# New instruction order and PSUM placement in the attention pass of a macaron layer (slot-routed FFN, delta-rule attention, FFN again)

## Chip, cores and metric

One core of a Trainium2 chip. The metric is the device time of the whole program in microseconds (us).

## What is computed

`x` is (2, 4096, 512), all float32. Three stages, of which the kernel makes three passes:

```python
x = x + 0.5 * ffn(layernorm(x))     # FFN: 64 slots, top-8 routing, a GRU step on the slots
x = x + attention(layernorm(x))       # 16 heads of 32; below x is the normed tile
x = x + 0.5 * ffn(layernorm(x))
# attention, 16 heads of 32, for every position t:
q, k = l2norm(x @ Wq), l2norm(x @ Wk);  v = x @ Wv
alpha, beta = sigmoid(x @ Wa + ba), sigmoid(x @ Wb + bb)
state = alpha * state + outer(k, beta * (v - k @ state));  y = q @ state
y = rmsnorm(y, g_norm) * silu(x @ Wg);  return y @ Wo
```

The kernel does the attention in chunks of 32 positions (the four chunks of a 128-row tile side by side on the partitions), with a 32x32 unit-triangular matrix per head and chunk that is inverted on VectorE, and one 32x32 state product per head from chunk to chunk. Note: the pass also adds the first FFN's output to x before attention, and does the routing of the second FFN (its layer norm, logits, top 8, slot sums) behind it.

## The kernel before

Rows are taken in 32 tiles of 128 positions for each of the 2 batches; a function's arguments are (tile n, batch b, part). There are four stretches: routing of the first FFN (to about 309.7 us), the attention pass (309.7 to about 2880 us), a short GRU stage (`mid`), and the last sum with the output.

The attention pass is software-pipelined over tiles and its order is written out by hand, one list for each engine: a fill (`first_pe`, `first_act`, `first_pool`, `first_dve`, `first_sp`), a steady step called once per tile, and a drain (`last_...`). Engines meet only through semaphores, and each runs its own list strictly in order. A step works on tile p (adding the FFN, transposing, projecting), on q = p - 1 (32x32 products and inversion), on r = q - 1 (state chain, output product, second routing) and on s = r - 1 (slot sums). What matters for the steps below:

- TensorE, 128-wide products: `proj_k`, `proj_q` (4 parts each per batch, one 128x512 product a part, L899 through `project`), `proj_va` (keys of 128x288), `proj_vb`, `proj_g` (L954), `out_proj` (L1101), `hidden`, `ffn` (L886), `slots`, `qe_T`, transposes.
- TensorE, 32x32 products, always 16 of them to a piece and 4 of them side by side in the array: `gram` (L994), `apply_uw` (L1018), `apply_gy` (eight pieces for each batch; a half with 8 products on L1060, which waits for `gq_turn`, and a half with 8 products on L1069, which waits for `y1_turn`), `chain` (L1082, four links for each batch). In the trace each float32 product stands as two matmul records, so a half of an `apply_gy` piece is x16.
- ScalarE copies results out of PSUM: `move_uw` (L2166) after `apply_uw`, `move_gq` (L2172) after the fourth and the eighth piece of `apply_gy`, `move_va`, squares, `gate_of`.
- VectorE: `chunk_kept` (L3280) after `move_gq`; `state` (L3286), the transpose between two chain links; `query_scale` (L3225), `reading` (L3254), `invert` (L3267 and L3269, 30 rounds in ten calls), `first_sum` (L3168), `second_sum` (L3297, reads the output product), `last_top` and `last_weights` (routing).
- GpSimd: masks, decays, norms' powers, `slot_add` (L2718).
- The sync engine's queue (SP): the matrix to be inverted goes out to DRAM and comes back in another layout (`coupling_out`, `coupling_in`), the inverse likewise (`inverse_out` L531, `inverse_in` L537, from which `apply_uw` reads); `load_alpha` (L494) brings the routing weights for `ffn`.

PSUM has 8 banks of 128x512; each result has a bank (the lists `..._at`), and `free(...)` in front of a product waits until the last reader of that bank's previous content is done. Thus `proj_va(n, 0)` writes bank 3, which `out_proj(n-2, 1)` had, and waits for `x2`, the signal of `second_sum(n-2, 1)`:

```python
if part == 0:
    pe.wait_ge(S["xnT"], both(n, b))
    if b == 0:
        free((n - 2, (S["x2"], both(n - 2, 1))), (n - 1, (T["pt"][1], nth(n - 1, 1))))
```

In the steady list before, the pieces of `apply_gy` of batch 0 stand as six at the end of a step and two at the start of the next, with nothing between them.

Of the kernel before, what the change touches and what calls it, by code (L numbers as in the profile page):

```python
# [3876 lines left out]
```

How the kernel before makes its waits and increments, by code:

```python
            def __call__(self, ins):  # L238
                ins.then_inc(self.sem, 1)
                self.n += 1
                self.e.wait_ge(self.sem, self.base + self.n)
# [99 lines left out]
        def mid(e, m):  # L341
# [10 lines left out]
                def gate_product(dst, j, c, n):  # L352
                    for k in range(KC):
                        if j == 0 and k % 2 == 0:
                            e.wait_ge(mid_act, o_act + 1 + k // 2)
                        last = mm(dst, giT[:, k * P:(k + 1) * P], wihT_at(k, j)[:, c:c + n], start=(k == 0), stop=(k == KC - 1))
                    last.then_inc(mid_pe, 1)
                def value(k):
                    return mm(Bk[1][:, :], hTT[:, k * P:(k + 1) * P], voT_at(k), start=(k == 0), stop=(k == KC - 1))
                e.wait_ge(mid_dve, o_dve + 1)
                turn(0)
                e.wait_ge(mid_dve, o_dve + 2)
                turn(1)
                if m == 1:
                    e.wait_ge(wih_in, RELOAD)
                gate_product(A[0][:, :], 0, 0, D)
                e.wait_ge(aT, NT * (m + 1))
                gate_product(C[0][:, :], 2, 0, D)
                gate_product(z_at[0], 1, 0, HC)
                gate_product(z_at[1], 1, HC, HC)
                e.wait_ge(mid_dve, o_dve + 7)
                turn(0)
                e.wait_ge(mid_act, o_act + 7)
                value(0)
                e.wait_ge(mid_dve, o_dve + 8)
                turn(1)
                value(1)
                e.wait_ge(mid_act, o_act + 8)
```

## Time and profile before

| | |
|---|---|
| median of 3 runs | 2947.53 us (2940.21 to 2959.49) |
| span of the profiled execution | 2958.8 us |
| slowest of the 3 runs | 2959.49 us |
| TensorE matmul busy | 2700.6 us (91%) |
| VectorE, ScalarE, GpSimd busy | 1882.3, 1059.9, 1328.6 us |
| attention pass, first to last `ffn` product | 309.7 to 2706.5 us |

The span runs from the first to the last instruction of one execution; 2959.49 us is the run that stands nearest to it, 0.7 us above, and the profile does not name a time of its own beside the span. A row of a group of instructions gives line, engine, operation, output and inputs, shape and count, then busy time, mean length of one (ns), and the engine's idle time just before them with what ended it; "issue" is idle time for which the profile shows no cause.

### The profile page before, as it was taken

What the parts mean: (1) busy time and instruction counts of PE and PEld (TensorE: products, weight loads), DVE (VectorE), ACT (ScalarE), POOL (GpSimd) and SP (SyncE); (2) the same over time, 40 slices, a digit from 0 to 9 for tenths busy, and PEclk for the clock granted to TensorE, in tenths of its full rate; (3) what the DMA queues carried; (4) which work ended last, traced back from release to release, by engine and by line L of the source; (5) the groups of instructions that cost most, each with busy time, mean ns of one, the idle gap of its engine ahead of it and who ended that gap; (6) DMA issues with size and microseconds to landing.
All of it is one profiled execution on the core that took longest, in us unless ns stands there. A gap on an engine that the chain in (4) does not pass through costs nothing. (4 is left out here: it accounts for less than half of the span.)

```text
span 2958.8 us, 117088 instructions
## 1 busy us (share of the span) xinstructions
PE 2700.6 (91%) x51052; PEld 1927.0 (65%) x51052; DVE 1882.3 (64%) x5306; ACT 1059.9 (36%) x1964; POOL 1328.6 (45%) x1767
## 2 busy tenths in 40 slices
PE   7999889899999999999999999999999999999867
PEld 5887556566666666666666666666666666666653
DVE  6777456566666666666666666666666666665626
ACT  5777223333333333333333333333333333333220
POOL 2222444445545444444554545555554444455410
PEclk9999999999999999999999999999999999999988
DMA  7352112211122222212222222212222222122178
GB/s 234 94 162 65 42 49 61 59 49 46 56 60 61 61 61 61 60 56 54 58 58 58 60 61 59 57 49 54 58 58 61 61 61 61 54 55 60 46 250 309
DMA packets 365965, 224.78 MB, mean 76 GB/s; under 512 B 277584, under 2 KB 294032, under 8 KB 365456
## 3 DMA queue, kind: packets, MB, share of 16 engines
q1 hardware_dynamic: 356240, 200.51, 24.0%
q10 hardware_dynamic: 9216, 16.78, 1.5%
q8 instruction: 405, 6.64, 0.9%
q14 instruction: 104, 0.85, 0.1%
HBM read 125.49 MB, written 74.97 MB: 68 GB/s over the span
## 5 line engine op out<-in xcount | busy, mean ns | idle before, releaser
L899 PE MATMUL psum<-w_all,xnT 128*128 128x512 f32 (+2 forms) x2048 | 732.6, 501 | 41.5 <-DVE xh L3297 33.9
L2602 POOL TENSOR_TENSOR sm<-sm,half 128x1 f32<-128x1 f32 (+1 forms) x384 | 535.3, 1394 | 85.1 <-ACT sm L2149 69.1
L899 PEld LDWEIGHTS psum<-w_all,xnT 128*128 128x128 f32 x2048 | 372.2, 190 | 285.7 <-issue 235.5
L3269 DVE TENSOR_TENSOR blk<-blk 128x30 f32<-128x30 f32 (+14 forms) x960 | 382.3, 398 | 33.0
L3267 DVE TENSOR_TENSOR blk<-blk 128x30 f32<-128x30 f32 (+14 forms) x960 | 369.8, 385 | 40.0 <-issue 14.2
L954 PE MATMUL psum<-xnT,w_all 128*128 128x128 f32 x2048 | 264.4, 281 | 0.9 <-DVE xc L3168 0.9
L1069 PE MATMUL psum<-pk,uw 32*32 32x64 f32 x8192 | 221.6, 216 | 44.3 <-issue 44.2
L1101 PE MATMUL psum<-w_out,gate 128*128 128x512 f32 x512 | 253.0, 613 | 5.4 <-DVE gate L3291 3.6
L954 PEld LDWEIGHTS psum<-xnT,w_all 128*128 128x128 f32 x2048 | 245.4, 193 | 16.6 <-issue 6.3
L1060 PE MATMUL psum<-pk,uw 32*32 32x64 f32 x8192 | 226.4, 221 | 24.9 <-issue 23.0
L1060 PEld LDWEIGHTS psum<-pk,uw 32*32 32x32 f32 x8192 | 141.6, 104 | 116.6 <-issue 101.3
L1082 PEld LDWEIGHTS psum<-qg,st 32*32 32x32 f32 x8192 | 131.8, 106 | 124.6 <-issue 63.5
L2642 POOL TENSOR_SCALAR sm<-sm 128x1 f32<-128x1 f32 x64 | 16.2, 253 | 435.2 <-DVE sm L3302 435.2
L2634 POOL TENSOR_SCALAR sm<-sm 128x1 f32<-128x1 f32 x64 | 14.5, 227 | 428.5 <-DVE sm L3174 428.3
L1082 PE MATMUL psum<-qg,st 32*32 32x64 f32 x8192 | 174.7, 219 | 31.8 <-DVE st L3286 18.6
L1069 PEld LDWEIGHTS psum<-pk,uw 32*32 32x32 f32 x8192 | 149.3, 105 | 54.6 <-issue 50.4
L2172 ACT ACTIVATE qg<-psum 128x256 f32<-128x256 f32 x128 | 48.7, 380 | 359.8 <-PE psum L1060 359.6
L3286 DVE STREAM_TRANSPOSE st<-psum 128x128 f32<-128x128 f32 x256 | 80.8, 316 | 128.0 <-PE psum L1082 124.6
L994 PEld LDWEIGHTS psum<-kqT 32*32 32x32 f32 x8192 | 124.9, 106 | 48.3 <-issue 41.2
L994 PE MATMUL psum<-kqT 32*32 32x64 f32 x8192 | 144.6, 217 | 10.9 <-issue 9.5
L1018 PEld LDWEIGHTS psum<-vk,E 32*32 32x32 f32 x8192 | 123.6, 105 | 38.6 <-issue 33.9
L1018 PE MATMUL psum<-vk,E 32*32 32x64 f32 x8192 | 140.8, 215 | 5.4 <-issue 2.8
(278 smaller groups left out, 4662.6 us busy)
## 6 DMA issues: line engine op xcount, KB each, us to landing
blk<-n_scratch SPq DMA_DIRECT2D x64, 512.0 KB, 4.4
xin<-in_L_attn_x_dram SPq DMA_DIRECT2D x96, 256.0 KB, 2.8
xh<-xc SPq DMA_DIRECT2D x64, 256.0 KB, 2.3
n_scratch<-nn SPq DMA_DIRECT2D x64, 256.0 KB, 3.6
e_scratch<-blk SPq DMA_DIRECT2D x32, 512.0 KB, 2.6
E<-e_scratch SPq DMA_DIRECT2D x64, 256.0 KB, 3.2
x_scratch<-xh SPq DMA_DIRECT2D x62, 256.0 KB, 2.3
rxn<-in_L_attn_x_dram SPq DMA_DIRECT2D x32, 256.0 KB, 3.0
```

What stands on the lines that cost most here:

```text
L899: last = mm(dst, xnT[b][:, k * P:(k + 1) * P], w_all[:, k * WK + at:k * WK + at + n], start=(k == 0), stop=(k == KC - 1))
L954: last = mm(g_at[b][:, part * P:(part + 1) * P], w_all[:, at:at + P], xnT[b][:, k * P:(k + 1) * P], start=(k == 0), stop=(k == KC - 1))
L994: last = mm(q32(gram_at[b][part], c, at, 2 * HD), q32(kqT[b], c, h * 2 * HD, HD), q32(kqT[b], c, h * 2 * HD, 2 * HD), start=True, stop=True)
L1018: last = mm(q32(uw_at[b][part], c, at, 2 * HD), q32(E[b], c, h * HD, HD), vk3[b][CH * c:CH * (c + 1), n % 2::2 - n % 2, h, :], start=True, ...
L1060: last = mm(q32(gq_at[b][part], hq, (k * NC + c) * 2 * HD, 2 * HD), q32(uw[b], c, at + HD, HD), q32(pk[b], c, at, 2 * HD), start=False, st ...
L1069: last = mm(q32(y_at[b], hq, ((2 * part + k) * NC + c) * 2 * HD, 2 * HD), q32(uw[b], c, at, HD), q32(pk[b], c, at, 2 * HD), start=(k == 0 ...
L1082: last = mm(q32(y_at[b], hq, at, 2 * HD), q32(st[b], hq, x * P + hb * HD, HD), q32(qg[b], hq, at, 2 * HD), start=False, stop=True, skip_gr ...
L1101: last = mm(wo_at[b], gate[b][:, part * P:(part + 1) * P], w_out[:, part * D:(part + 1) * D], start=(part == 0), stop=(part == KC - 1))
L2602: return g.tensor_tensor(dst, a, half[:, 0:n], ALU.pow)
L3267: own(tt(o, Y[:, 0:rows, s_:s_ + 1].to_broadcast([P, rows, cols]), N[:, s_:s_ + 1, s_ + 1:CH].to_broadcast([P, rows, cols]), ALU.mult))
L3269: ins = tt(Y[:, 0:rows, s_ + 1:CH], Y[:, 0:rows, s_ + 1:CH], o, ALU.add)
L3286: v.transpose(st[b][:, (c % 2) * P:(c % 2 + 1) * P].rearrange("p (k e) -> p k e", k=KC), new).then_inc(scp[b], 1)
```

## The change

Every function of the attention pass issues the same instructions as before; what changes is the order of the calls on all five engines, the bank of each PSUM tile, and with the banks the `free(...)` waits. The fill is shorter: the steady step now begins at t = 4 and not at t = 6, and runs to t = 31 and not 30. The step gets an argument o = p + 1, used by SP alone (`load_alpha` one tile further ahead).

Banks:

```diff
-        k_at = [banks(7, 1), banks(1, 1)]
-        q_at = [banks(2, 1), banks(0, 1)]
-        va_at = [banks(3, 1), banks(4, 1)]
-        vb_at = [banks(2, 1), banks(1, 1)]
-        wo_at = [banks(0, 1), banks(3, 1)]
-        y_at = [banks(3, 2), banks(6, 2)]
-        uw_at = [[banks(7, 1), banks(3, 1)], [banks(1, 1), banks(4, 1)]]
-        gq_at = [[banks(6, 1), banks(5, 1)], [banks(2, 1), banks(5, 1)]]
...
+        k_at = [banks(4, 1), banks(2, 1)]
+        q_at = [banks(5, 1), banks(3, 1)]
+        va_at = [banks(0, 1), banks(7, 1)]
+        vb_at = [banks(3, 1), banks(6, 1)]
+        wo_at = [banks(2, 1), banks(3, 1)]
+        y_at = [banks(4, 2), banks(4, 2)]
+        uw_at = [[banks(4, 1), banks(7, 1)], [banks(7, 1), banks(6, 1)]]
+        gq_at = [[banks(1, 1), banks(6, 1)], [banks(0, 1), banks(6, 1)]]
```

Some of the waits that go with them, in `proj_va`, `ffn` and the first piece of `apply_gy`:

```diff
-                        free((n - 2, (S["x2"], both(n - 2, 1))), (n - 1, (T["pt"][1], nth(n - 1, 1))))
+                        free((n - 2, (S["yv"], both(n - 2, 1))), (n, (S["x1"], both(n, 0))))
...
-                free((n - 2, (S["x2"], both(n - 2, 0))), (n - 1, (S["qn"], both(n - 1, 1))))
+                free((n - 2, (T["qg"][1], nth(n - 2, 0))), (n - 1, (S["va"], both(n - 1, 0))))
+                free((n - 3, (S["slc"], n - 3)), (n - 2, (S["yv"], both(n - 2, 0))), (n - 1, (T["pt"][0], nth(n - 1, 0))))
...
+                            free((n, (T["uw"][0], nth(n, 0))))
+                            free((n + 1, (S["qn"], both(n + 1, 0))), (n - 1, (S["ysq"], both(n - 1, 1))))
```

The new steady step of TensorE:

```diff
+            def step_pe(o, p, q, r, s):
+                apply_gy(r, 0, 5)
+                apply_gy(r, 0, 6)
+                proj_q(q, 1, 2)
+                proj_q(q, 1, 3)
+                apply_gy(r, 0, 7)
+                gram(q, 0, 0)
+                gram(q, 0, 1)
+                chain(r, 0, 0)
+                qe_T(r, 1, 0)
+                dec(q, 0)
+                chain(r, 0, 1)
+                chain(r, 0, 2)
+                gram(q, 0, 2)
+                cum(q)
+                chain(r, 0, 3)
+                dec(q, 1)
+                gram(q, 0, 3)
+                gram(q, 1, 0)
+                gram(q, 1, 1)
+                apply_uw(r, 1, 0)
+                apply_uw(r, 1, 1)
+                out_proj(r, 0, 0)
+                out_proj(r, 0, 1)
+                gram(q, 1, 2)
+                gram(q, 1, 3)
+                apply_gy(r, 1, 0)
+                y_norm(r, 0)
+                out_proj(r, 0, 2)
+                out_proj(r, 0, 3)
+                apply_gy(r, 1, 1)
+                apply_uw(r, 1, 2)
+                apply_gy(r, 1, 2)
+                apply_uw(r, 1, 3)
+                apply_gy(r, 1, 3)
+                slots(s)
+                qe_T(r, 1, 1)
+                apply_gy(r, 1, 4)
+                apply_gy(r, 1, 5)
+                apply_gy(r, 1, 6)
+                apply_gy(r, 1, 7)
+                ffn(p)
+                proj_g(q, 1, 0)
+                chain(r, 1, 0)
+                chain(r, 1, 1)
+                proj_g(q, 1, 1)
+                chain(r, 1, 2)
+                proj_vb(q, 1, 0)
+                proj_vb(q, 1, 1)
+                chain(r, 1, 3)
+                last_xT(r, 0)
+                proj_g(q, 0, 0)
+                proj_g(q, 0, 1)
+                proj_g(q, 0, 2)
+                proj_g(q, 1, 2)
+                proj_g(q, 0, 3)
+                out_proj(r, 1, 0)
+                out_proj(r, 1, 1)
+                out_proj(r, 1, 2)
+                proj_g(q, 1, 3)
+                y_norm(r, 1)
+                out_proj(r, 1, 3)
+                first_xT(p, 0)
+                hidden(r, 0, 0)
+                hidden(r, 0, 1)
+                proj_k(p, 0, 0)
+                alpha_T(s)
+                proj_q(p, 0, 0)
+                logits(r, 0)
+                proj_va(p, 0, 0)
+                proj_k(p, 0, 1)
+                proj_k(p, 0, 2)
+                last_xT(r, 1)
+                proj_k(p, 0, 3)
+                proj_va(p, 0, 1)
+                hidden(r, 1, 0)
+                proj_q(p, 0, 1)
+                hidden(r, 1, 1)
+                proj_vb(p, 0, 0)
+                proj_vb(p, 0, 1)
+                logits(r, 1)
+                proj_q(p, 0, 2)
+                first_xT(p, 1)
+                proj_q(p, 0, 3)
+                qe_T(q, 0, 0)
+                proj_va(p, 1, 0)
+                proj_va(p, 1, 1)
+                proj_k(p, 1, 0)
+                proj_k(p, 1, 1)
+                qe_T(q, 0, 1)
+                proj_k(p, 1, 2)
+                proj_q(p, 1, 0)
+                apply_uw(q, 0, 0)
+                apply_uw(q, 0, 1)
+                apply_uw(q, 0, 2)
+                apply_uw(q, 0, 3)
+                proj_k(p, 1, 3)
+                apply_gy(q, 0, 0)
+                apply_gy(q, 0, 1)
+                apply_gy(q, 0, 2)
+                apply_gy(q, 0, 3)
+                proj_q(p, 1, 1)
+                apply_gy(q, 0, 4)
```

Of ScalarE:

```diff
+            def step_act(o, p, q, r, s):
+                move_uw(r, 0, 1)
+                last_exp(s, 1)
+                move_gq(r, 0, 1)
+                query_square(q, 1)
+                dec_exp(q, 0)
+                y_square(r, 0)
+                decay_exp(q)
+                dec_exp(q, 1)
+                move_uw(r, 1, 0)
+                y_mean(r, 0)
+                move_gq(r, 1, 0)
+                move_uw(r, 1, 1)
+                last_normal(r, 0)
+                slot_copy(s)
+                move_gq(r, 1, 1)
+                first_normal(p, 0)
+                move_vb(q, 1)
+                last_move(r, 0)
+                gate_of(q, 0)
+                y_square(r, 1)
+                y_mean(r, 1)
+                gate_of(q, 1)
+                move_xT(p, 0)
+                last_gelu(r, 0)
+                last_normal(r, 1)
+                last_aT(s)
+                last_move(r, 1)
+                last_gelu(r, 1)
+                key_square(p, 0)
+                first_normal(p, 1)
+                move_vb(p, 0)
+                move_xT(p, 1)
+                query_square(p, 0)
+                gates_exp(p)
+                move_va(p, 0)
+                last_exp(r, 0)
+                gates_ln(p)
+                move_va(p, 1)
+                move_uw(q, 0, 0)
+                move_gq(q, 0, 0)
+                key_square(p, 1)
```

Of VectorE:

```diff
+            def step_dve(o, p, q, r, s):
+                key_turn(q, 0)
+                query_scale(q, 0)
+                key_sums(q, 1)
+                query_turn(q, 0)
+                chunk_kept(r, 0, 0)
+                chunk_kept(r, 0, 1)
+                query_sums(q, 1)
+                key_scale(q, 1)
+                state(r, 0, 0)
+                key_turn(q, 1)
+                state(r, 0, 1)
+                state(r, 0, 2)
+                query_scale(q, 1)
+                query_turn(q, 1)
+                state(r, 0, 3)
+                coupling(q, 0, 0)
+                reading(q, 0, 0)
+                gated(r, 0)
+                coupling(q, 0, 1)
+                last_weights(s, 1)
+                coupling(q, 1, 0)
+                coupling(q, 1, 1)
+                reading(q, 0, 1)
+                second_sum(r, 0)
+                last_moments(r, 0)
+                reading(q, 1, 0)
+                chunk_kept(r, 1, 0)
+                reading(q, 1, 1)
+                chunk_kept(r, 1, 1)
+                invert(q, 1, 4)
+                first_sum(p, 0)
+                state(r, 1, 0)
+                first_moments(p, 0)
+                state(r, 1, 1)
+                invert(q, 4, 7)
+                state(r, 1, 2)
+                invert(q, 7, 10)
+                state(r, 1, 3)
+                gated(r, 1)
+                invert(q, 10, 13)
+                invert(q, 13, 16)
+                second_sum(r, 1)
+                last_moments(r, 1)
+                invert(q, 16, 19)
+                invert(q, 19, 22)
+                first_sum(p, 1)
+                invert(q, 22, 25)
+                first_moments(p, 1)
+                invert(q, 25, 28)
+                invert(q, 28, 31)
+                key_sums(p, 0)
+                last_top(r, 0)
+                last_top(r, 1)
+                query_sums(p, 0)
+                gates_in(p)
+                gates_beta(p)
+                key_scale(p, 0)
+                gates_decay(p)
+                last_weights(r, 0)
```

Of SP, and the part of GpSimd's that the text speaks of:

```diff
+            def step_sp(o, p, q, r, s):
+                load_first(p, 0)
+                inverse_in(r, 0)
+                inverse_in(r, 1)
+                coupling_out(q, 0)
+                load_first(p, 1)
+                coupling_out(q, 1)
+                store_second(r, 0)
+                coupling_in(q)
+                hold(q, 0)
+                store_second(r, 1)
+                hold(q, 1)
+                inverse_out(q)
+                store_alpha(s)
+                load_alpha(o)
...
+            def step_pool(o, p, q, r, s):
+                query_decayed(r, 1)
+                beta_mask(q, 0)
+                decay_rows(q, 0)
+                decay_rows(q, 1)
+                key_power(q, 1)
+                query_power(q, 1)
+                decay_mask(q, 0)
+                y_pairs(r, 0)
+                beta_mask(q, 1)
+                decay_mask(q, 1)
+                chunk_decay(q, 0)
+                y_power(r, 0)
+                last_rstd(r, 0)
+                alpha_sums(s)
+                key_written(q, 0)
+                chunk_decay(q, 1)
+                key_decayed(q, 0)
+                slot_add(s)
+                first_rstd(p, 0)
+                y_pairs(r, 1)
+                query_decayed(q, 0)
+                y_power(r, 1)
+                last_rstd(r, 1)
+                key_written(q, 1)
+                first_rstd(p, 1)
+                key_power(p, 0)
+                query_power(p, 0)
+                key_decayed(q, 1)
```

## Rows read from the trace of the kernel before

**Rows 1.** The page: span, busy time, instruction queue (packets, MB, share of 16 engines)
```profile
span 2958.8 us, 117088 instructions
...
PE 2700.6 (91%) x51052; PEld 1927.0 (65%) x51052; DVE 1882.3 (64%) x5306; ACT 1059.9 (36%) x1964; POOL 1328.6 (45%) x1767
...
q8 instruction: 405, 6.64, 0.9%
```

**Rows 2.** Busy time by stretch: length, PE, PEld, DVE, ACT, POOL, clock, DMA, GB/s
```profile
501.90:592.60 90.70, 80.58 (x1577) 55.66 (x1575) 54.65 (x149) 27.42 (x50) 46.22 (x58) 0.96 0.20 53
669.80:2553.10 1883.30, 1755.53 (x36652) 1244.47 (x36650) 1207.12 (x3242) 633.98 (x1152) 943.01 (x1200) 0.99 0.22 58
...
2800.00:2958.80 158.80, 116.92 (x1391) 70.94 (x1379) 75.29 (x176) 28.48 (x55) 14.52 (x28) 0.87 0.73 260
```

**Rows 3.** Groups of TensorE's instructions by line and shape, whole span
```profile
L1060 PE MATMUL psum<-pk,uw 32*32 32x64 f32 x8192 | 226.4, 221 | 24.9 <-issue 23.0 <-ACT vk L2134 1.1 <-ACT uw L2166 0.7
L1069 PE MATMUL psum<-pk,uw 32*32 32x64 f32 x8192 | 221.6, 216 | 44.3 <-issue 44.2
L1082 PE MATMUL psum<-qg,st 32*32 32x64 f32 x8192 | 174.7, 219 | 31.8 <-DVE st L3286 18.6 <-issue 11.6 <-DVE qg L3280 1.4
...
L899 PE MATMUL psum<-w_all,xnT 128*128 128x288 f32 x512 | 140.6, 416 | 34.7 <-DVE xh L3297 33.9 <-ACT xnT L2105 0.7
...
L886 PE MATMUL psum<-sv,aT_in 64*128 64x512 f32 x128 | 39.8, 688 | 13.9 <-DMA aT_in<-alphaT_scratch 13.2 <-DVE sv L3150 0.8
```

**Rows 4.** TensorE in order of time, a run of `apply_gy` pieces of batch 0
```profile
1500.08 0.43 PE L1060 MATMUL psum<-pk,uw 32*32 32x64 f32 x16
1500.33 0.40 PE L1069 MATMUL psum<-pk,uw 32*32 32x64 f32 x16
1500.59 0.43 PE L1060 MATMUL psum<-pk,uw 32*32 32x64 f32 x16
...
1502.24 0.42 PE L1069 MATMUL psum<-pk,uw 32*32 32x64 f32 x14
1503.61 0.21 PE L1069 MATMUL psum<-pk,uw 32*32 32x64 f32 x1 [0.94 <-issue]
```

**Rows 5.** TensorE in order of time: chain links of the last tile, nothing between them
```profile
2861.51 0.65 PE L1082 MATMUL psum<-qg,st 32*32 32x64 f32 x32 [0.44 <-DVE st L3286]
```

**Rows 6.** Groups of ScalarE's instructions in one step, 1500 to 1578.4 us
```profile
L2166 ACT ACTIVATE uw<-psum 128x512 f32<-128x512 f32 x4 | 2.4, 597 | 2.0 <-PE psum L1018 2.0
...
L2172 ACT ACTIVATE qg<-psum 128x256 f32<-128x256 f32 x4 | 1.5, 379 | 12.3 <-PE psum L1060 12.3
```

**Rows 7.** Groups of VectorE's instructions in the same step
```profile
L3267 DVE TENSOR_TENSOR blk<-blk 128x30 f32<-128x30 f32 (+14 forms) x30 | 11.8, 395 | 2.3 <-issue 1.5
...
L3286 DVE STREAM_TRANSPOSE st<-psum 128x128 f32<-128x128 f32 x8 | 2.5, 316 | 3.3 <-PE psum L1082 3.2
L3280 DVE TENSOR_TENSOR qg<-psum,qa 128x256 f32<-128x256 f32 x4 | 1.7, 420 | 2.7 <-ACT qg L2172 2.7
...
L3168 DVE TENSOR_TENSOR xc<-xin,psum 128x512 f32<-128x512 f32 x2 | 1.4, 686 | 0.1
```

**Rows 8.** All engines in order of time: an inversion round beside a GpSimd operation
```profile
1548.44 0.40 DVE L3269 TENSOR_TENSOR blk<-blk 128x234 f32<-128x234 f32 x1
...
1549.22 1.04 POOL L2696 TENSOR_TENSOR qa<-qs,gt 128x512 f32<-128x512 f32 x1
...
1549.32 1.21 DVE L3269 TENSOR_TENSOR blk<-blk 128x238 f32<-128x238 f32 x1
```

**Rows 9.** The DMA queue of SP in order of time: the inverse's way
```profile
1567.32 0.33 SPq L531 DMA_DIRECT2D e_scratch<-blk  x1
1569.97 1.75 SPq L537 DMA_DIRECT2D E<-e_scratch  x2
```

**Rows 10.** The page's DMA issues: KB each, us from issue to landing
```profile
xin<-in_L_attn_x_dram SPq DMA_DIRECT2D x96, 256.0 KB, 2.8
...
E<-e_scratch SPq DMA_DIRECT2D x64, 256.0 KB, 3.2
```

More of the change, by code:

```diff
@@ L1560, in first_pe @@
                 apply_gy(1, 0, 3)
+                proj_q(2, 1, 1)
+                apply_gy(1, 0, 4)
+                apply_gy(1, 0, 5)
+                apply_gy(1, 0, 6)
+                proj_q(2, 1, 2)
+                proj_q(2, 1, 3)
+                apply_gy(1, 0, 7)
+                gram(2, 0, 0)
+                gram(2, 0, 1)
+                chain(1, 0, 0)
+                qe_T(1, 1, 0)
+                dec(2, 0)
+                chain(1, 0, 1)
+                chain(1, 0, 2)
+                gram(2, 0, 2)
@@ L1594, in first_pe @@
                 apply_gy(1, 1, 3)
+                qe_T(1, 1, 1)
                 apply_gy(1, 1, 4)
                 apply_gy(1, 1, 5)
-                ffn(3)
                 apply_gy(1, 1, 6)
                 apply_gy(1, 1, 7)
+                ffn(3)
+                proj_g(2, 1, 0)
+                chain(1, 1, 0)
+                chain(1, 1, 1)
+                proj_g(2, 1, 1)
+                chain(1, 1, 2)
+                proj_vb(2, 1, 0)
+                proj_vb(2, 1, 1)
+                chain(1, 1, 3)
@@ L2376, in first_act @@
                 move_xT(2, 1)
[L2377 to L2384 removed]
+                query_square(2, 0)
+                gates_exp(2)
+                move_va(2, 0)
+                gates_ln(2)
+                move_va(2, 1)
+                move_uw(1, 0, 0)
+                move_gq(1, 0, 0)
@@ L3312, in last_dve @@
             def last_dve():
-                key_sums(NT - 2, 1)
-                chunk_kept(NT - 3, 0, 0)
-                query_turn(NT - 2, 0)
-                last_top(NT - 4, 1)
-                key_scale(NT - 2, 1)
-                key_turn(NT - 2, 1)
-                last_weights(NT - 4, 0)
-                chunk_kept(NT - 3, 0, 1)
-                query_sums(NT - 2, 1)
-                state(NT - 3, 0, 0)
-                state(NT - 3, 0, 1)
-                state(NT - 3, 0, 2)
-                query_scale(NT - 2, 1)
@@ L3474, in last_dve @@
                 invert(NT, 28, 31)
-                second_sum(NT - 1, 1)
-                last_moments(NT - 1, 1)
+                last_top(NT - 1, 0)
+                last_top(NT - 1, 1)
+                last_weights(NT - 1, 0)
                 chunk_kept(NT, 0, 0)
-                last_top(NT - 1, 0)
                 chunk_kept(NT, 0, 1)
@@ L3668, in first_dve @@
-                key_sums(4, 1)
-                key_turn(4, 0)
-                query_turn(4, 0)
-                last_weights(2, 0)
-                key_scale(4, 1)
-                chunk_kept(3, 0, 0)
-                query_sums(4, 1)
-                last_top(2, 1)
-                key_turn(4, 1)
-                query_scale(4, 1)
-                chunk_kept(3, 0, 1)
-                state(3, 0, 0)
-                state(3, 0, 1)
-                query_turn(4, 1)
-                state(3, 0, 2)
```

1939 lines of the change are left out of this document (413 added, 1526 removed).

## Prediction

> **What bounds the kernel now.** I read the page first: matmuls are busy for 2700.6 of the 2958.8 us span, 91%, and no other engine above 64% [rows 1]. So the kernel is as long as TensorE's list, plus what that list waits for. The table by stretch then gives the size of a step. The steady part, taken from one tile's `ffn` to that of the tile 24 later, lasts 1883.3 us, which is 78.5 us a step, of which matmuls are busy for 73.1; the step before it, from tile 4 to tile 5, lasts 90.7 us and is still part of the fill [rows 2]. The change issues the same products, and by my count the old and the new step both pass 13 times from 32x32 products to 128-wide ones and back, so what a change of form costs is paid equally often. TensorE's pure work in a step is then unchanged, and only its waits can move.
>
> The groups by line say what those waits are [rows 3]. Four kinds: `proj_va` of batch 0 waits for `second_sum` (33.9 us in the pass, nearly once a step); `ffn` waits for its weights' DMA (13.2 us); the chain waits for the transpose on VectorE (18.6 us); and the 32x32 products stand still for "issue", for which no engine or DMA is responsible: 23.0 on L1060, 44.2 on L1069 and 11.6 us on L1082. In order of time one sees what this last kind looks like. A piece of `apply_gy` starts 0.51 us after the last (1500.08, 1500.59), several in a row; then, inside a piece, TensorE sits for 0.94 us, and resumes in the middle of it [rows 4]. Such a stop falls into runs of small products, and I take it for late instructions: a half piece is 16 loads and 16 matmuls in 0.25 us, while a part of a projection is 4 instructions in some 0.86, and the kernel draws its instructions through a DMA queue of its own in 405 packets of 16 KB [rows 1].
>
> The Trainium skill ("Runtime: NRT & Kernel Launch", section "Instruction fetch mechanics") says that instructions are refilled in blocks of 256, and also that the fetch is hidden because dispatch is slower than the refill. Rows 4 speak against the second half; the stops may yet have another cause, and this rule is a rival below.
>
> **What the new order removes, per step.**
> (a) The wait of `proj_va(p, 0)`. It is there because that product's bank is the one that `second_sum(r, 1)` still reads; the new bank 0 was last read by `y_mean` and `first_sum`, both long before. 33.9 us over the some 27 steps that have it is 1.25 us [rows 3]; some of it may come back where `proj_vb(p, 0)` now uses that reader's bank, but this stands about 10 us later in the list. I take 1.2, bounds 0.6 and 1.25.
> (b) The wait of `ffn`. `load_alpha` is now issued a tile earlier. 13.2 us over 32 tiles: 0.4 us.
> (c) Stops for "issue". In the old list eight pieces of `apply_gy` of batch 0 stand in one run, 512 and more instructions; in the new one they stand as 4, 3 and 1 with projection products between them. The runs of batch 1, four or five pieces long, stay about as they are. L1060 and L1069 lose 67.2 us, 2.1 us a tile [rows 3], and I give half to batch 0, which has the long run. I take 1.0; bounds 0 (the stop only moves to the next small products) and 2.1.
> (d) The chain's waits, 18.6 us over 32 tiles, 0.6 us; they are replaced by (e) and (f).
> Together 3.2 us.
>
> **What it adds, per step.**
> (e) Links 1 and 2 of the chain of batch 0 now stand next to one another. With nothing between them the second one waits 0.44 us for the transpose [rows 5]. 0.44, if VectorE is free just then: its list has `state(r, 0, 1)` and `state(r, 0, 2)` next to one another too.
> (f) Links 0 and 1 of batch 1 also stand together, and here VectorE isn't free. Count from the start of the last piece `apply_gy(r, 1, 7)`. TensorE's way: the piece with the change of form 0.7, `ffn` 1.1, `proj_g` 1.0, link 0 0.45: it wants link 1 at 3.2 us. VectorE's way: the first half's result 0.43 [rows 4], `move_gq` 0.38 [rows 6], `chunk_kept` 0.42 [rows 7], hand-overs 0.15, then `invert(q, 1, 4)`, then `first_sum(p, 0)` 0.69, then the transpose 0.32. The three rounds of that `invert` would take 2.4 at the mean of 0.395 for each instruction [rows 7]; they are among the narrowest and I take 1.4. Sum 3.8, with a hand-over 3.9: link 1 waits 0.7. Beside it GpSimd comes to `slot_add`, and rounds of the inversion beside a GpSimd operation can take 1.21 instead of 0.40 us [rows 8]; that is up to 0.8 more. I take 1.0; bounds 0.44 and 1.8. The skill ("SBUF — State Buffer") has a rule for this, an exclusive port pair on which the loser fully blocks; the trace agrees, and it changes nothing in the sum.
> (g) `apply_gy(q, 0, 4)` needs the second `move_uw` of batch 0, which ScalarE now does after `move_gq(q, 0, 0)` and `key_square(p, 1)`. From the start of piece 3: 0.43 until its first half is there, `move_gq` 0.38, two 128x512 activations of 0.60 [rows 6], hand-overs 0.1: 2.1 us. TensorE is there after the piece, one `proj_q` and the changes of form: 0.5 + 0.86 + 0.35, 1.7. Wait 0.4; I take 0.3, bounds 0 and 0.6.
> (h) `apply_gy(q, 0, 0)` now writes the banks that `key_scale` and `query_scale` of the tile p read. VectorE has 1207.12/24 = 50.3 us of work a step [rows 2]. About 38 of it, 23.6 of them inversion [rows 7], lie between `chunk_kept(r, 1, 1)` and `query_scale`, since both `last_top` and a `last_weights` moved into this stretch; with 3.5 us of waiting for ScalarE's exp and log and for the output product it is 42 us, and TensorE's list needs 43 between the same two points. So it is hidden with 1 us to spare, less than my sums are good for. I take 0.3, bounds 0 and 2.5. Without that cover every us on VectorE is a us of the step.
> (i) The inverse's way: from `e_scratch` (issue 2.65 us before the next, [rows 9]) and 3.2 us to land for `E` [rows 10], some 6.5 us; SP now issues `load_alpha` and a 256 KB load in between. TensorE wants the result about 7.5 us after VectorE ends: hidden, by 1 us. 0 in the sum, bounds 0 and 2.
> Together 2.0 us, so a step gets 1.2 us shorter, 77.3 us, and 27 of them give 32 us. The fill's last step of 90.7 us [rows 2] becomes a steady one: 13 us. The drain after 2800 us has 158.8 us with 116.92 busy; its waits are chains of single operations of the last tile that keep their order, and I leave them.
>
> **Sum.** 45 us off. The span of 2958.8 becomes 2914; that execution is close to the slowest of the three runs (2959.49), 0.4% above the median, and the median becomes 2947.5 - 45 = 2902 us. A measurement of this kernel tells about 1% from no change, 29 us.
>
> **Rivals.**
> A. The inversion's engine becomes the bound (h, i). For it: a margin of 1 us in a step of 77, and GpSimd operations that lengthen single rounds threefold [rows 8]. Against it: VectorE is busy for 50.3 of 78.5 us now. With 1.0 us more in (h) the step is 78.3 and only the fill is gained: 2935 us. Chance 0.22.
> B. No gain in (c), by the skill's rule that the fetch is hidden. Then the stops belong to the single product and follow it wherever it stands: step 78.3 too, with (h) as summed, 2930 us. For it: the profile names no releaser. Against it: the pieces before the stop run at 0.51 us each. Chance 0.08.
> C. The gain in (c) is whole, 2.1, for TensorE's new waits (e) to (g) also give the fetch time, and (f) costs only 0.44. The step is 75.6, 27 times 2.9 is 78, with the fill 91: 2856 us. Chance 0.15.
> D. Slower. One mechanism: the inverse comes late for `apply_uw(q, 0, 0)`, because two loads are ahead of `inverse_in` in SP's queue; if these delay it by their 2.8 us [rows 10] and VectorE ends its rounds 1.5 us later than now through (h), the 1 us of cover is gone and 3.3 are on the path. It decides from 2.2 us of added delay (then the 1.2 gained are used up). Step 80.6, 27 times 2.1 is 57, less the fill's 13: 2992 us. Chance 0.11.
>
> **How the numbers follow.** My forecast has 0.44, with its own range from 2875 to 2925. Faster by over 1% (below 2918) holds most of it (0.39), C (0.15) and little of A and B (0.04): 0.58. Within 1% hold the rest of the forecast, of A and of B: 0.30. Slower is D and the tail of A: 0.12. The range leaves out half of D and a fifth of C: 2848 to 2975.
>
> **What would show it.** Right: no idle time of `proj_va` for `xh` and of `ffn` for `aT_in`; issue stops on L1060 and L1069 down from 67 to about 35 us; link idle time on L1082 for `st` up from 18.6 to about 40 us; a step of 77.3 us between `ffn` products, from tile 4 on. Wrong: L1060 waiting for `qs` or `xh`-like names of VectorE (A), L1018 waiting for `E` (D), issue stops of 67 us as before (B) or below 15 (C).

## The result: 1.3% slower, and the profile after

The changed kernel takes 2996.18 us (median of 4 runs, 2985.76 to 3004.96), the kernel before beside it 2953.51 us (4 runs). The ratio is 1.0126, 95% interval [1.0095, 1.0158]: slower, where I forecast 2902 us. The page of the changed kernel:

```profile
span 2983.5 us, 117215 instructions
...
PE 2726.1 (91%) x51052; PEld 1952.7 (65%) x51052; DVE 1869.4 (63%) x5306; ACT 1041.1 (35%) x1962; POOL 1326.6 (44%) x1767
```

The span has grown by 24.7 us, and TensorE's busy time by 25.5 us [rows 1], with the same 51052 matmuls. The mean granted clock fell from 0.985 to 0.961. The groups of TensorE's instructions, by line and shape (L849 is the old L899, L1011 and L1020 are L1060 and L1069, L1033 is L1082, L970 is L1018, L836 is L886):

```profile
L849 PE MATMUL psum<-w_all,xnT 128*128 128x512 f32 x1024 | 515.4, 608 | 3.0 <-ACT xnT L1715 2.4 <-issue 0.6
L906 PE MATMUL psum<-xnT,w_all 128*128 128x128 f32 x2048 | 280.2, 294 | 3.2 <-issue 3.2
L1011 PE MATMUL psum<-pk,uw 32*32 32x64 f32 x8192 | 228.9, 221 | 18.7 <-issue 13.4 <-ACT uw L1776 3.8
L1020 PE MATMUL psum<-pk,uw 32*32 32x64 f32 x8192 | 226.0, 217 | 34.2 <-issue 33.1
L1033 PE MATMUL psum<-qg,st 32*32 32x64 f32 x8192 | 186.8, 232 | 98.6 <-DVE st L2646 95.2 <-issue 2.1 <-DVE qg L2640 1.1
L970 PE MATMUL psum<-vk,E 32*32 32x64 f32 x8192 | 151.7, 218 | 15.8 <-issue 13.0 <-DMA E<-e_scratch 2.6
L849 PE MATMUL psum<-w_all,xnT 128*128 128x288 f32 x512 | 141.7, 410 | 0.0
L836 PE MATMUL psum<-sv,aT_in 64*128 64x512 f32 x128 | 41.2, 706 | 5.5 <-issue 4.8 <-DVE sv L2510 0.8
```

Against [rows 3]: the wait of the 128x288 product is gone (34.7 to 0.0), so is that of `ffn` for `aT_in`; "issue" on the pieces' two lines fell from 67.2 to 46.5 us; and the chain's wait for `st` rose from 18.6 to 95.2 us. The last number is five times what it was. Where it falls one sees in order of time, in a step of the middle. First TensorE, then VectorE, then GpSimd:

```profile
1537.76 0.72 PE L906 MATMUL psum<-xnT,w_all 128*128 128x128 f32 x5
1538.41 0.65 PE L1033 MATMUL psum<-qg,st 32*32 32x64 f32 x32
1542.91 1.08 PE L1033 MATMUL psum<-qg,st 32*32 32x64 f32 x32 [3.85 <-DVE st L2646]
1543.92 2.08 PE L906 MATMUL psum<-xnT,w_all 128*128 128x128 f32 x8
```
```profile
1538.64 0.15 DVE L2627 TENSOR_TENSOR blk<-blk 128x30 f32<-128x30 f32 x1 [1.41 <-issue]
...
1538.83 1.01 DVE L2629 TENSOR_TENSOR blk<-blk 128x30 f32<-128x30 f32 x1
1539.87 1.22 DVE L2627 TENSOR_TENSOR blk<-blk 128x58 f32<-128x58 f32 x1
1541.13 0.22 DVE L2629 TENSOR_TENSOR blk<-blk 128x58 f32<-128x58 f32 x1
...
1541.94 0.69 DVE L2528 TENSOR_TENSOR xc<-xin,psum 128x512 f32<-128x512 f32 x1
1542.55 0.31 DVE L2646 STREAM_TRANSPOSE st<-psum 128x128 f32<-128x128 f32 x1
```
```profile
1537.37 1.05 POOL L2136 TENSOR_TENSOR qa<-gt,eye 128x512 f32<-128x512 f32 x1 [2.54 <-DVE qg L2640]
1538.38 0.28 POOL L2150 TENSOR_SCALAR sm<-gt 128x16 f32<-128x16 f32 x1
1538.75 1.05 POOL L2152 TENSOR_TENSOR vk<-kn,sm 128x512 f32<-128x512 f32 x1
1539.75 1.26 POOL L2180 TENSOR_TENSOR slotacc<-slotacc,slt 128x512 f32<-128x512 f32 x1
```

Link 0 of batch 1 runs at 1538.41. Link 1 can't start before VectorE's transpose of 1542.55, and that stands in VectorE's list behind `invert(q, 1, 4)` and `first_sum`. An inversion round is two such operations, L2627 and L2629. Two of the six of this `invert` take 1.01 and 1.22 us where their neighbours take 0.15 to 0.25, and they are those beside GpSimd's `key_decayed` (L2152) and `slot_add` (L2180). `chunk_decay` (L2136) was released by the same `qg` product behind which VectorE begins its inversion. Over the 24 steady steps the median of this `invert` is 3.98 us, and link 1 waits 3.1 us in the median, 2.6 on average.

The windows of this trace show what the wait does to what follows (length, then busy time of PE, PEld, DVE, ACT and POOL, granted clock, DMA share, GB/s):

```profile
1536.30:1541.00 4.70, 2.76 (x48) 1.72 (x44) 3.05 (x6) 0.26 (x1) 3.54 (x4) 1.00 0.31 105
1541.00:1544.40 3.40, 1.49 (x34) 1.32 (x35) 2.82 (x10) 0.00 (x0) 0.60 (x4) 0.54 0.03 5
1544.40:1547.80 3.40, 3.40 (x42) 2.91 (x42) 2.24 (x9) 0.81 (x1) 0.73 (x2) 0.50 0.00 0
1547.80:1551.20 3.40, 3.40 (x50) 2.78 (x50) 2.66 (x8) 0.90 (x2) 0.00 (x0) 0.96 0.00 0
664.40:2570.50 1906.10, 1776.58 (x36656) 1261.15 (x36650) 1197.01 (x3240) 620.84 (x1153) 941.87 (x1200) 0.97 0.22 58
585.60:664.40 78.80, 73.28 (x1531) 51.89 (x1528) 50.08 (x135) 25.58 (x48) 39.15 (x50) 0.98 0.20 49
```

Clock 1.00 until 1541.0; within the wait it falls, and it stays at 0.50 (1.2 GHz) while TensorE is busy all the time from 1544.4 to 1547.8. The same link that takes 0.65 us takes 1.08, and the one part of `proj_g` behind it (8 matmul records) takes 2.08, where it takes 1.16 us at full clock (at 1465.11 us). Counted over the 24 steady steps, the changed kernel has 24 such stretches, in 20 of the steps, 4.5 us a step; the kernel before has 4, 0.85 us a step. It fits that L1033's matmuls grew from 219 to 232 ns each though they are the same.

The steady rows give the balance. 24 steps took 1883.3 us with 1755.5 busy [rows 2]; now 1906.1 with 1776.6. Idle time a step is 5.32 and 5.40 us: the order took out as much as it put in. Busy time a step is 73.15 and 74.02 us: +0.88. Together +0.95 us a step, 22.8 us in 24 steps; the part ahead of them is 5.4 us shorter (664.4 against 669.8) and the part behind 7.3 longer (413.0 against 405.7). That is the 24.7 us of the span.

### The profile page after: what moved, and what is told of

Read it like the earlier page. It is cut to its first block, busy times and chain, and to the rows that moved or that the text cites. A ratio compares the mean times of both kernels' runs of the same rounds, so it can differ in the third digit from the quotient of the medians.

```text
span 2983.5 us, 117215 instructions
## 1 busy us (share of the span) xinstructions
PE 2726.1 (91%) x51052; PEld 1952.7 (65%) x51052; DVE 1869.4 (63%) x5306; ACT 1041.1 (35%) x1962; POOL 1326.6 (44%) x1767
## 4 chain that ended last, share of the span: by engine, by line
PE 81%; DVE 10%; issue 5%; ACT 2%; DMA 1%; SPq 1%; POOL 1%; DVEq 0%; ACTq 0%; POOLq 0%
PE psum L849 22%; PE psum L1052 8%; PE psum L906 7%; PE psum L1011 5%; PE psum L1033 5%; PE psum L970 4%; PE psum L946 4%; PE psum L1020 4%; PE psum L1073 4%; PE psum L690 3%; DVE blk L2627 2%; PE psum L989 2%; PE psum L753 2%; DVE blk L2629 2%; PE psum L927 2%
## 5 line engine op out<-in xcount | busy, mean ns | idle before, releaser
L849 PE MATMUL psum<-w_all,xnT 128*128 128x512 f32 (+2 forms) x2048 | 774.8, 509 | 3.0 <-ACT xnT L1715 2.4
L849 PEld LDWEIGHTS psum<-w_all,xnT 128*128 128x128 f32 x2048 | 364.8, 195 | 147.2 <-issue 97.4
L2627 DVE TENSOR_TENSOR blk<-blk 128x30 f32<-128x30 f32 (+14 forms) x960 | 375.4, 391 | 49.5 <-issue 23.9
L2629 DVE TENSOR_TENSOR blk<-blk 128x30 f32<-128x30 f32 (+14 forms) x960 | 351.6, 366 | 33.0
L906 PEld LDWEIGHTS psum<-xnT,w_all 128*128 128x128 f32 x2048 | 262.4, 206 | 49.2 <-issue 47.5
L906 PE MATMUL psum<-xnT,w_all 128*128 128x128 f32 x2048 | 280.2, 294 | 3.2 <-issue 3.2
L1033 PE MATMUL psum<-qg,st 32*32 32x64 f32 x8192 | 186.8, 232 | 98.6 <-DVE st L2646 95.2
L1020 PE MATMUL psum<-pk,uw 32*32 32x64 f32 x8192 | 226.0, 217 | 34.2 <-issue 33.1
L2163 POOL TENSOR_TENSOR sq<-sq 128x256 f32<-128x256 f32 x64 | 47.4, 741 | 453.8 <-ACT sq L1795 453.8
L1011 PE MATMUL psum<-pk,uw 32*32 32x64 f32 x8192 | 228.9, 221 | 18.7 <-issue 13.4
L1033 PEld LDWEIGHTS psum<-qg,st 32*32 32x32 f32 x8192 | 140.9, 114 | 160.6 <-DVE st L2646 131.0
L1011 PEld LDWEIGHTS psum<-pk,uw 32*32 32x32 f32 x8192 | 142.9, 105 | 131.0 <-issue 93.1
L1020 PEld LDWEIGHTS psum<-pk,uw 32*32 32x32 f32 x8192 | 153.8, 105 | 46.1 <-issue 40.4
L970 PE MATMUL psum<-vk,E 32*32 32x64 f32 x8192 | 151.7, 218 | 15.8 <-issue 13.0
L2657 DVE SCALAR_TENSOR_TENSOR xh<-psum,sm,xh 128x512 f32<-128x512 f32 x64 | 48.0, 751 | 180.2 <-PE psum L1052 180.2
L970 PEld LDWEIGHTS psum<-vk,E 32*32 32x32 f32 x8192 | 128.7, 106 | 43.3 <-issue 40.0
L1710 ACT ACTIVATE xn<-xc,sm 128x512 f32<-128x512 f32 x64 | 52.2, 816 | 289.1 <-POOL sm L2099 289.0
L2614 DVE TENSOR_TENSOR pk<-psum,dm 128x256 f32<-128x256 f32 x128 | 53.2, 417 | 156.6 <-PE psum L1020 156.6
```

The lines of the kernel that those rows point to most:

```text
L849: last = mm(dst, xnT[b][:, k * P:(k + 1) * P], w_all[:, k * WK + at:k * WK + at + n], start=(k == 0), stop=(k == KC - 1))
L906: last = mm(g_at[b][:, part * P:(part + 1) * P], w_all[:, at:at + P], xnT[b][:, k * P:(k + 1) * P], start=(k == 0), stop=(k == KC - 1))
L970: last = mm(q32(uw_at[b][part], c, at, 2 * HD), q32(E[b], c, h * HD, HD), vk3[b][CH * c:CH * (c + 1), n % 2::2 - n % 2, h, :], start=True, ...
L1011: last = mm(q32(gq_at[b][part], hq, (k * NC + c) * 2 * HD, 2 * HD), q32(uw[b], c, at + HD, HD), q32(pk[b], c, at, 2 * HD), start=False, st ...
L1020: last = mm(q32(y_at[b], hq, ((2 * part + k) * NC + c) * 2 * HD, 2 * HD), q32(uw[b], c, at, HD), q32(pk[b], c, at, 2 * HD), start=(k == 0 ...
L1033: last = mm(q32(y_at[b], hq, at, 2 * HD), q32(st[b], hq, x * P + hb * HD, HD), q32(qg[b], hq, at, 2 * HD), start=False, stop=True, skip_gr ...
```

## The experiments

My theory after the result: (1) link 1 of batch 1 is late because its transpose stands behind an inversion call that three GpSimd operations lengthen; (2) the half clock after that wait costs about as much again as the wait. The rivals: the change of form or the late instructions cost the time, and the wait only happens to be there. Twelve kernels ran, four at a time on one chip, each time with the kernel before. That kernel took 2984.14, 2950.52 and 2970.81 us on the three chips, so ratios are compared, and medians only within one set.

**Set 1: four ways to take the wait away.** k1 changes VectorE's list alone:

```diff
 chunk_kept(r, 1, 1)
-invert(q, 1, 4)
 first_sum(p, 0)
 state(r, 1, 0)
 first_moments(p, 0)
 state(r, 1, 1)
+invert(q, 1, 4)
 invert(q, 4, 7)
```

> Of the changed kernel, in VectorE's step only: first_sum, both state transposes of batch 1 and first_moments stand ahead of invert(q, 1, 4). Theory 1 (link 1 of batch 1's chain waits because three inversion rounds, lengthened by GpSimd, stand ahead of its transpose, and the idle TensorE is then given the lower clock): idle time of the chain's line for the transpose falls from 95 us to about 30, the mean granted clock rises from 0.961 to about 0.98, the step from 79.4 to about 75.5 us, the kernel from 2996 to about 2890 us. Theory 2 (VectorE's whole list is the bound, and the wait is only where it shows): the wait moves to second_sum's or query_scale's readers and the kernel stays within 1% of 2996 us, or gets slower, since VectorE now idles 2 us a step for the chain.

k2 changes GpSimd's list alone:

```diff
+first_rstd(p, 0)
 chunk_decay(q, 1)
 key_decayed(q, 0)
 slot_add(s)
-first_rstd(p, 0)
```

> Of the changed kernel, in GpSimd's step only: chunk_decay(q, 1), key_decayed(q, 0) and slot_add(s) go behind first_rstd(p, 0), so they no longer run beside the first inversion rounds. If GpSimd lengthens the rounds (2.6 us of the wait), the first call of the inversion falls from 3.95 to about 1.4 us, the wait of link 1 from 2.5 to about 0.7 us a step, and the kernel comes to about 2910 us. If the rounds are long for another reason (late matrix, late instructions), the first call stays near 4 us and so does the kernel near 2996 us.

k3 has both edits.

> Both edits. Theory 1: little beyond the better of the two, about 2885 us; GpSimd's operations then lengthen rounds that nobody waits for. If each removes a wait of its own, it is some 30 us below the better of the two.

k4 leaves VectorE and GpSimd as changed and puts 128-wide products of TensorE's list between the links:

```diff
 chain(r, 1, 0)
-chain(r, 1, 1)
 proj_g(q, 1, 1)
-chain(r, 1, 2)
 proj_vb(q, 1, 0)
 proj_vb(q, 1, 1)
-chain(r, 1, 3)
+chain(r, 1, 1)
 last_xT(r, 0)
 proj_g(q, 0, 0)
+chain(r, 1, 2)
 proj_g(q, 0, 1)
+chain(r, 1, 3)
```

> Of the changed kernel, in TensorE's step only: one part of proj_g and both of proj_vb, 2.9 us of work, go between links 0 and 1 of batch 1, and wide products between the later links. VectorE and GpSimd as they are. Theory 1: the transpose is as late as before, but TensorE has work meanwhile, so nearly all of the wait (2.5 us a step) and of the lower clock goes: about 2890 us. Theory 2 (VectorE's list is the bound): no gain, about 2990 us.

Measured ("steady step" is the mean in us of the 23 steps from tile 5 to tile 28, "wait" the chain's idle time for `st` in the pass, "half clock" the time at half clock in such a step):

| kernel | median us | ratio to before, 95% | steady step | wait | half clock |
|---|---|---|---|---|---|
| k1 | 2934.95 | 0.9837 [0.9816, 0.9858] | 77.1 | 59.5 | 1.3 |
| k2 | 2931.03 | 0.9821 [0.9805, 0.9837] | 77.7 | 45.6 | 2.7 |
| k3 | 3040.92 | 1.0187 [1.0155, 1.0219] | 80.6 | 123.3 | 4.6 |
| k4 | 2916.97 | 0.9776 [0.9761, 0.979] | 76.6 | 27.8 | 1.6 |

Three edits that have only the late link in common each end 1.6 to 2.2% below the time of before, from a kernel that was 1.1 to 1.3% above it. VectorE in k2, and the link that it releases:

```profile
1595.70 0.19 DVE L2629 TENSOR_TENSOR blk<-blk 128x30 f32<-128x30 f32 x1
1595.92 0.22 DVE L2627 TENSOR_TENSOR blk<-blk 128x58 f32<-128x58 f32 x1
```
```profile
1599.42 0.65 PE L1033 MATMUL psum<-qg,st 32*32 32x64 f32 x32 [0.44 <-DVE st L2646]
```

The two operations that took 1.01 and 1.22 us take 0.19 and 0.22 without GpSimd beside them, and the whole `invert` takes 1.45 us in every steady step. In k4 it is as long as in the changed kernel (median 3.87 us), but link 1 waits only 0.3 us a step. k1 kept more waiting than I expected (59.5 us, not 30): link 1 waits 0.66 us a step and link 3 now 0.69. (1) is shown, and so is that either half of it suffices: the order on VectorE, or GpSimd's operations beside it. Had the change of form been the cost, k1 and k2, which leave TensorE's list alone, would have stayed at 1.01.

k3 is the useful miss. Each edit alone gains, both together, from which I expected the fastest of the three, are some 3.6% slower than either. Its trace: TensorE's third wait of the step, then VectorE, then GpSimd.

```profile
1569.51 0.65 PE L1033 MATMUL psum<-qg,st 32*32 32x64 f32 x32 [3.18 <-DVE st L2646]
```
```profile
1564.29 1.12 DVE L2629 TENSOR_TENSOR blk<-blk 128x84 f32<-128x84 f32 x1
...
1565.75 1.06 DVE L2629 TENSOR_TENSOR blk<-blk 128x108 f32<-128x108 f32 x1
1566.84 1.24 DVE L2627 TENSOR_TENSOR blk<-blk 128x130 f32<-128x130 f32 x1
...
1569.14 0.32 DVE L2646 STREAM_TRANSPOSE st<-psum 128x128 f32<-128x128 f32 x1
```
```profile
1562.92 0.23 POOL L2096 TENSOR_SCALAR sm<-sm 128x1 f32<-128x1 f32 x1 [7.42 <-DVE sm L2534]
...
1564.26 1.04 POOL L2136 TENSOR_TENSOR qa<-gt,eye 128x512 f32<-128x512 f32 x1
1565.28 0.27 POOL L2150 TENSOR_SCALAR sm<-gt 128x16 f32<-128x16 f32 x1
1565.63 1.05 POOL L2152 TENSOR_TENSOR vk<-kn,sm 128x512 f32<-128x512 f32 x1
1566.64 1.29 POOL L2180 TENSOR_TENSOR slotacc<-slotacc,slt 128x512 f32<-128x512 f32 x1
```

The moved operations met the moved calls again, one place further on: `invert(q, 1, 4)` and `invert(q, 4, 7)` now stand together before the transpose that link 3 needs, three of their operations take 1.06 to 1.24 us, and link 3 waits 3.2 us (median) instead of link 1. The two edits together bring this about: k2's puts the three operations behind `first_rstd`, which waits for `first_moments` (L2534), and k1's puts `first_moments` directly ahead of the two calls. It is the same mechanism at another link, at a like price.

**Set 2: the portions and the clock.** k5 is k4 with the eight pieces of batch 0 in one run again:

```diff
+proj_q(p, 1, 1)
 apply_gy(q, 0, 0)
...
 apply_gy(q, 0, 3)
-proj_q(p, 1, 1)
 apply_gy(q, 0, 4)
...
 apply_gy(r, 0, 6)
+apply_gy(r, 0, 7)
 proj_q(q, 1, 2)
 proj_q(q, 1, 3)
-apply_gy(r, 0, 7)
```

> The kernel of k4_fill_gap with one thing of the kernel before given back: the eight pieces of batch 0's matrix products with gy stand in one run again instead of in pairs among the products of q. Theory (instructions come late in long dense runs of small products, and the portions were worth 1.0 us a step in the sum): idle time after issue on the pieces' two lines grows from k4's 54 us by about 28 us, the step from 76.7 to about 77.7 us, ratio about 0.987 of the kernel before. Rival B (late instructions are only moved, portions are worth nothing): ratio 0.978 as k4, idle after issue over all lines within 5 us of k4's.

k6 is k4 with one wide product more in batch 1's run:

```diff
 apply_gy(r, 1, 5)
+proj_g(q, 1, 0)
 apply_gy(r, 1, 6)
 apply_gy(r, 1, 7)
 ffn(p)
-proj_g(q, 1, 0)
-chain(r, 1, 0)
 proj_g(q, 1, 1)
+chain(r, 1, 0)
```

> The kernel of k4_fill_gap with the run of small products in batch 1 broken by one proj_g between its pieces 5 and 6, and another proj_g moved ahead of link 0. Theory (late instructions in dense runs): the stops in pieces 5 to 7 of batch 1 shrink, 0.5 to 1.0 us a step, ratio about 0.970. Rival (the stops move to the next place): ratio 0.978, the same idle after issue.

k7 is the changed kernel with three dummy products in the gap, and k8 the changed kernel itself:

```diff
+def filler(b):
+    for _ in range(3):
+        mm(g_at[0], xnT[b][:, 0:P], w_all[:, W_K:W_K + D], start=True, stop=True)
...
 chain(r, 1, 0)
+filler(1)
 chain(r, 1, 1)
```

> The changed kernel with three additional products of 128x512 between links 0 and 1 of batch 1, into a PSUM bank that is overwritten afterwards; the output is unchanged and nothing waits for them, so that TensorE is busy while link 1's operand is late, and the operand comes no earlier. Theory (half of the loss is the clock that falls after the wait): the stretches at half clock disappear from most of the 23 middle steps that show one, the step falls from 79.5 to about 77.6 us, 45 to 50 us less than k8 as a whole, ratio about 0.997 of the kernel before. Rival (the wait alone costs): the step stays at 79.5 us, ratio as k8's, 1.013.

> The changed kernel as it is, on the chip of the other runs, as their base: ratio 1.013 of the kernel before, link 1 of batch 1 late by some 3 us, and one stretch at half clock in nearly every step.

| kernel | median us | ratio to before, 95% |
|---|---|---|
| k5 | 2912.50 | 0.9864 [0.9821, 0.9908] |
| k6 | 2903.61 | 0.9835 [0.9791, 0.9879] |
| k7 | 2966.32 | 1.0043 [1.0016, 1.0069] |
| k8 | 2983.99 | 1.0110 [1.0058, 1.0163] |

k8 repeats the result. k7 issues more work and does all the rest as k8, and its median is 17.7 us lower: the intervals of the two ratios just overlap, but each of k7's ten runs is below each of k8's four. The two profiled executions lie only 3.9 us apart. The steady windows of 24 steps of k8, then of k7, and k7's groups (L1026 are the dummies, L1037 the chain):

```profile
748.20:2637.60 1889.40, 1772.31 (x36654) 1261.25 (x36650) 1194.75 (x3240) 620.30 (x1153) 940.39 (x1200) 0.97 0.22 58
```
```profile
747.70:2631.00 1883.30, 1803.65 (x36801) 1257.05 (x36792) 1198.14 (x3240) 620.90 (x1153) 942.18 (x1200) 0.99 0.22 58
```
```profile
L1037 PE MATMUL psum<-qg,st 32*32 32x64 f32 x8192 | 175.6, 223 | 33.5 <-DVE st L2651 25.7 <-issue 6.5 <-DVE qg L2645 1.2
L1026 PE MATMUL psum<-w_all,xnT 128*128 128x512 f32 x168 | 79.9, 610 | 0.1
```

TensorE is busy 73.85 us a step in k8 and 75.15 in k7. Of the latter the dummies are 2.85 (79.9 us over the 28 steps that have them), so the kernel's own products take 72.30: 1.55 us a step less for the same products. The stretches at half clock fell from 21 to 4 in 23 steps (4.45 to 0.89 us a step). So the clock's share is shown, and it is the price of the half clock in the changed kernel: about 1.5 us a step. The size of k7's gain I had wrong, 18 instead of 45 to 50 us, because the idle time that the dummies took the place of came back in part: "issue" on L1011, L1020 and the chain grew from 42.2 us in k8 to 67.7.

k5's ratio is the one that the theory of late instructions gave (0.987), but not for its reason: "issue" on the pieces' two lines is 50.0 us against k4's 54.4, where the theory wanted 28 more, and what grew is the wait for `uw`, to 34.2 us. k6 came out above both of its forecasts (0.970 and 0.978). "Issue" on the two lines is 45.9 us there, but the edit isn't clean: with only `proj_vb` left between links 0 and 1 of batch 1, link 1 waits 1.0 us a step again.

k5 and k6 had run on another chip than k4, and by their ratios k4 is ahead of both, by their steps (76.5 and 76.3 us against 76.6) it isn't. So k4 and k5 ran again in the last set.

**Set 3: k4 and k5 side by side, and two attempts at the rest.**

> The kernel of k4_fill_gap once more, on the same chip as the kernel of k5_run_of_eight, since the two had run on different chips, whose runs of the kernel before lie 1.1% apart. This run and the next decide what the portions of batch 0's matrix products are worth. Theory (portions worth 1.0 us a step): some 28 us faster than k10. Rival B (worth nothing): within 6 us of k10. The traces so far (step 76.7 against 76.6 us) speak for the rival.

> The kernel of k5_run_of_eight once more, beside k9. Theory: 28 us slower than k9. Rival B: within 6 us of it; the run of eight then waits 1.2 us a step at its fifth piece for the eviction of uw, and the stops that the portions had are gone from behind it.

k11 is k6 with `gram(q, 0, 2)` moved ahead of `chain(r, 0, 2)`, and k12 is k11 with k1's order on VectorE.

> The kernel of k6_broken_run with one gram ahead of link 2 of batch 0, so that link 2 no longer stands right behind link 1. Theory: the wait of 0.44 us there goes, and the small product behind a wait was no switch more than before: step 76.3 to 75.9 us, about 12 us faster than k6's, ratio about 0.980 if k6's is 0.9835. Rival (stops behind it grow by what the wait gave): no change against k6.

> k11 with VectorE's order of k1_state_first (the inversion's first long call behind state of links 0 and 1 of batch 1). Theory: link 1's remaining wait of 1.0 us goes, some 25 us less than k11. Rival (as when both orders were mended together in k3_both): link 3's state is now late behind both calls of the inversion and the time grows by 20 us or more.

| kernel | median us | ratio to before, 95% |
|---|---|---|
| k9 (k4) | 2910.04 | 0.9801 [0.9768, 0.9835] |
| k10 (k5) | 2924.52 | 0.9849 [0.9809, 0.9889] |
| k11 | 2917.54 | 0.9818 [0.9790, 0.9847] |
| k12 | 2926.77 | 0.9852 [0.9832, 0.9873] |

k9 is 14.5 us ahead of k10, half of what the theory asked and more than the rival's 6; the intervals of the two ratios overlap. What makes the difference isn't what I thought. The pieces' lines of k9 and then of k10, and one piece of k10 in order of time:

```profile
L1011 PE MATMUL psum<-pk,uw 32*32 32x64 f32 x8192 | 230.3, 221 | 26.2 <-issue 20.8 <-ACT uw L1776 4.1
L1020 PE MATMUL psum<-pk,uw 32*32 32x64 f32 x8192 | 226.4, 217 | 29.0 <-issue 28.5
```
```profile
L1011 PE MATMUL psum<-pk,uw 32*32 32x64 f32 x8192 | 227.5, 221 | 52.0 <-ACT uw L1776 33.2 <-issue 18.2
L1020 PE MATMUL psum<-pk,uw 32*32 32x64 f32 x8192 | 223.1, 217 | 36.9 <-issue 36.5
```
```profile
1566.62 0.42 PE L1011 MATMUL psum<-pk,uw 32*32 32x64 f32 x16 [1.26 <-ACT uw L1776]
```

"Issue" differs by 5.4 us (49.3 against 54.7), less than between the two profiles of the changed kernel (46.5 and 38.7); the wait for ScalarE's eviction of `uw` differs by 29.1. In the run of eight the fifth piece comes before the second half of `uw`; the portions hold a projection product before it. That is cover for an eviction, and it isn't a saving in late instructions. The two are not fully told apart: the wait in k10 also gives late instructions time to arrive.

k11 (no change against k6's ratio) and k12 (k11 plus k1's edit, 9 us more, not 25 less) are both misses. In k11 the wait of 0.44 us ahead of link 2 of batch 0 became one of 0.11 us ahead of the `gram`, for another eviction by ScalarE; link 1 of batch 1 still waited 1.0. In k12 that wait was gone and link 3 of batch 1 waited 1.0 instead.

## Why the prediction was wrong

The step that failed is (f), and one cost that was in no step, the clock.

- (a) and (b) were right: 34.7 and 13.2 us of idle time are 0.0 for both.
- (c) gave 1.0 us a step for late instructions, from 67.2 to 35 us on the pieces' lines; it was 46.5, and 54.4 and 49.3 in the two runs of k4's kernel, where no long wait of the chain hides them. By place, "issue" ahead of batch 0's pieces fell from 1.26 to 0.36 us a step. But ahead of batch 1's pieces, its `apply_uw` and `ffn` it rose from 0.91 to 1.65 (1.35 in k8). The sentence that fell is that batch 1's runs stay about as they are. Why they rose is open; k6, with a wide product in that run, had 1.32. Over all lines "issue" fell from 3.20 to 2.22 us a step, as much as the 1.0 forecast, but that the portions did it isn't shown: with the run of eight restored (k5 and k10) batch 0's pieces had 0.17 and 0.21, no more than with the portions (0.34 and 0.24 in k4 and k9). The run of eight has its wait for `uw` in the middle, which may hide them too.
- (d) can't be read by itself: the chain's old waits for `st` are gone from their places, and (e) and (f) fill the same column.
- (e) was right: link 2 of batch 0 waits 0.44 us.
- (f) had the right mechanism and the wrong size: 1.0 taken, 1.8 as the upper bound, 2.6 measured (2.6 in k8 too). I took the three rounds of `invert` at 1.4 us plus up to 0.8 for one GpSimd operation. The 1.4 was right, as k2 shows (1.45); beside GpSimd it is 3.98, since `chunk_decay`, `key_decayed` and `slot_add` run back to back beside it. I had found `slot_add` there and didn't place the two ahead of it: they wait for the `qg` product that also precedes the inversion, so both lists start at one signal.
- (g) 0.3 taken, 0.13 measured; (h) 0.3 taken, no wait for `query_scale` among L1011's; (i) nothing taken, 0.1 measured (2.6 us in the pass). Rivals A and D rested on these and didn't come. A slower result did, by another way than D.
- The clock: in no step. Idle time a step went from 5.32 to 5.40 us, where I forecast 1.2 less; the rest of the miss is busy time, +0.88 us a step. The rows of before held no price for it: the granted clock is 0.99 over the steady part [rows 2], with 4 half-clock stretches in 24 steps, and TensorE's longest single wait there is 2.7 us, where the changed kernel has one of some 3 us in most steps.
- The fill was right in its one step: tile 4 to 5 took 79.3 us instead of 90.7. 4.4 us came back ahead of it (506.3 against 501.9).

Against the forecast of 77.3 us the step is 79.4: (f) is 1.6 of these 2.1 us, the clock 0.9, and the small terms (g) to (i) give some 0.4 back. With the late link alone mended (k4) the step is 76.6 and 75.9 us in its two runs; the forecast without the 1.0 of (f) is 76.3. So the rest of the sum stood as a whole, (c) for a reason that isn't shown.

The Trainium skill ("TensorE: Matmul & The Clock Gate", section "HAM oscillation — how this bites in real kernels") warns of waits between bursts of matmuls that throw the clock back each time round a loop. The trace agrees, in 20 of 24 steps and with 1.5 us of price a step, and I hadn't applied it to a wait of my own sum.

## What to carry to other kernels

Price a new wait of TensorE with what follows it: here some 2.6 us of waiting cost another 1.5 us at half clock, and filling the gap even with useless products paid. When two engines' lists are released by one signal, lay their next operations side by side and lengthen each by what its neighbour is, before a third engine's wait is summed; and check after each reordering where the same pairs meet next, as k3 shows. If the result of one small product is needed by the next, put products between them that need neither, rather than speed up the engine between.
